# A twelve-sublayer decoder on one core: the normalised tile of every layer norm made by ScalarE from a scale and an offset instead of by VectorE

## What is computed

```python
def _layernorm(x, axis=-1, eps=1e-05):
    m = jnp.mean(x, axis=axis, keepdims=True)
    v = jnp.var(x, axis=axis, keepdims=True)
    return (x - m) / jnp.sqrt(v + eps)
...
x = x + _L0_attn_ref(_layernorm(x, axis=-1), L0_attn_w_qkv, L0_attn_w_out)
x = x + _L0_xattn_ref(ctx_1024, ctx_1024, _layernorm(x, axis=-1), L0_xattn_Wk, ...)
x = x + _L0_ffn_ref(_layernorm(x, axis=-1), ...)
... (L1, L2 and L3 in the same way)
```

## Time and profile before

| | |
|---|---|
| three timed runs | 4872.91, 4877.81, 4878.98 us (median 4877.81) |
| the profiled execution, and its span | 4866.22 us, span 4864.2 us |
| PE busy | 3539.3 us, 73% |
| DVE busy | 2997.2 us, 62% |
| ACT busy | 2028.7 us, 42% |
| POOL busy | 1241.7 us, 26% |
| mean granted TensorE clock | 0.833 |

### The profile page before, as it was taken

One profiled execution on the slowest core, in us unless ns is written; L12 is line 12 of the kernel. 1 busy time (PEld: TensorE's weight loads), 2 busy tenths in 40 slices (PEclk: granted clock), 3 DMA queues, 4 the chain that ended last, 5 costly groups with the idle time before them and its releaser, 6 DMA issues. The chain is left out here.

```text
span 4864.2 us, 69143 instructions
## 1 busy us (share of the span) xinstructions
PE 3539.3 (73%) x25546; PEld 2352.9 (48%) x25546; DVE 2997.2 (62%) x7047; ACT 2028.7 (42%) x3183; POOL 1241.7 (26%) x1568
## 2 busy tenths in 40 slices
PE   6768868566977787764886887866588788686655
PEld 4645545334665454432574554533366455453333
DVE  4535873885553785577555488377655558737834
ACT  2324445343343444444343354544433354453422
POOL 0001450550000333254000044145200014505500
PEclk7979989768988898877997998977799899887666
DMA  6020021313211012222212002122312100213121
GB/s 222 7 92 20 27 76 40 128 38 104 85 58 61 31 45 83 70 81 78 98 45 102 12 27 79 44 89 74 106 55 80 66 18 28 85 36 120 40 100 46
DMA packets 174903, 327.99 MB, mean 67 GB/s; under 512 B 13260, under 2 KB 114988, under 8 KB 173740
## 3 DMA queue, kind: packets, MB, share of 16 engines
q1 hardware_dynamic: 174572, 323.59, 19.5%
HBM read 231.87 MB, written 91.67 MB: 67 GB/s over the span
## 5 line engine op out<-in xcount | busy, mean ns | idle before, releaser
L1980 POOL TENSOR_TENSOR sb_big<-sb_big 128x512 f32<-128x512 f32 x384 | 497.7, 1310 | 275.7 <-DVE sb_big L2080 275.6
L1417 POOL TENSOR_TENSOR sb_rs<-sb_ve,sb_weights_const 128x4 f32<-128x4 f32 x112 | 113.7, 1015 | 1635.7 <-DVE sb_ve L1403 1635.7
L1864 PE MATMUL bank<-sb_big,sb_weights_const 128*128 128x512 f32 x512 | 373.4, 819 | 202.0 <-DVE sb_big L2102 201.4
L1941 ACT ACTIVATE bank<-sb_big,sb_Aneg 128x512 f32<-128x512 f32 x512 | 350.5, 687 | 391.9 <-DVE sb_big L2097 272.3
L2097 DVE TENSOR_TENSOR_SCAN sb_big<-bank,sb_big 128x512 f32<-128x512 f32 x384 | 465.2, 1212 | 4.7 <-POOL sb_big L1980 4.7
L1235 DVE TENSOR_REDUCE sb_small<-bank 128x4 f32<-128x308 f32 (+1 forms) x512 | 265.1, 524 | 318.0 <-PE bank L950 311.7
L971 PE MATMUL bank<-sb_big 128*77 128x128 bf16 (+1 forms) x2560 | 359.3, 232 | 124.7 <-issue 85.5
L971 PEld LDWEIGHTS bank<-sb_big 128*77 128x77 bf16 (+1 forms) x2560 | 272.7, 116 | 213.3 <-issue 148.3
L1120 ACT ACTIVATE sb_big<-bank 77x512 f32<-77x512 f32 (+1 forms) x352 | 208.3, 593 | 263.3 <-PE bank L992 173.8
L974 PE MATMUL bank<-sb_topT,sb_pick 128*77 128x128 bf16 (+1 forms) x2048 | 301.7, 228 | 0.0
L950 PE MATMUL bank<-sb_big 128*128 128x77 bf16 (+1 forms) x2048 | 186.3, 226 | 155.6 <-DMA sb_big<-query_parts 98.8
(11 more groups left out here) (339 smaller groups left out, 8174.2 us busy)
## 6 DMA issues: line engine op xcount, KB each, us to landing
sb_big<-query_parts SPq DMA_DIRECT2D x160, 512.0 KB, 6.6
sb_big<-state_rows SPq DMA_DIRECT2D x128, 512.0 KB, 3.8
query_parts<-sb_big SPq DMA_DIRECT2D x120, 384.0 KB, 3.3
sb_big<-key_parts SPq DMA_DIRECT2D x64, 512.0 KB, 9.0
sb_big<-context_key_parts SPq DMA_DIRECT2D x64, 308.0 KB, 3.8
key_parts<-sb_big SPq DMA_DIRECT2D x48, 384.0 KB, 4.4
context_key_parts<-sb_big SPq DMA_DIRECT2D x48, 231.0 KB, 4.1
sb_big<-masked_key_parts SPq DMA_DIRECT2D x32, 308.0 KB, 3.5
```

Source lines behind the costliest of these rows:

```text
L1864: pe.matmul(m.bank[s][2][:, :], m.const["ident"], M.h(s, 2 * (n % 2)), start=n == 0, stop=n == NS - 1)\
L1941: act.activation(M.dA(s, half), M.dl(s, half), ACT.Exp, scale=m.Aneg[:, NS * half + n:NS * half + n + 1])\
L1980: pool.tensor_tensor(M.h(s, 2 * (n % 2) + half), M.b_rows(s, n // 2)[:, n % 2, :], M.du(s, half), ALU.mult)\
```

## The change

DVE no longer makes the normalised tile and no longer waits for POOL. It stops after variance + eps. POOL gets two small products per norm: before the power it multiplies the mean by -1 (`m.minus`, a new constant tile), and after it, it multiplies that by the reciprocal deviation; this wants a wait of POOL on its own power. ACT makes the tile with four `Identity` activations, with the reciprocal deviation as scale and the product as bias, both pointers to a column. They stand in ACT's queue at the due time at which DVE had them (0.01, and 0.03 for the inner norms). The signals of the quantised network now go by the experts' names (`ff_`), which frees semaphores and moves nothing; POOL's set-up gets a memset and a wait.

```diff
-    yield 0.01 if made is None else 0.03
-    dve.wait_ge(*g.at("ln_rstd", key))
-    for b in range(NB):
-        last = dve.tensor_scalar(dst[s][:, b, :], src[s][:, b, :], m.mv[s][:, b, 0:1], m.rs[s][:, b:b + 1],
-                                 ALU.subtract, ALU.mult)
-    last.then_inc(*g.one("ln_xn", key))
 
 
 def norm_pool(pool, g, m, key):
     s = g.s
     yield 0.03 if key in (k + "i" for k in NESTED) else 0.01
+    pool.wait_ge(*g.at("ln_aggr", key))
+    pool.tensor_tensor(m.nm[s][:, :], m.mv[s][:, :, 0], m.minus[:, :], ALU.mult)
     pool.wait_ge(*g.at("ln_var", key))
     pool.tensor_tensor(m.rs[s][:, :], m.ve[s][:, :], m.const["neghalf"], ALU.pow)\
         .then_inc(*g.one("ln_rstd", key))
+    pool.wait_ge(*g.at("ln_rstd", key))
+    pool.tensor_tensor(m.nm[s][:, :], m.nm[s][:, :], m.rs[s][:, :], ALU.mult)\
+        .then_inc(*g.one("ln_off", key))
+
+
+def norm_act(act, g, m, key, src, dst, made=None):
+
+    s = g.s
+    yield 0.01 if made is None else 0.03
+    act.wait_ge(*g.at("ln_off", key))
+    for b in range(NB):
+        last = act.activation(dst[s][:, b, :], src[s][:, b, :], ACT.Identity, bias=m.nm[s][:, b:b + 1],
+                              scale=m.rs[s][:, b:b + 1])
+    last.then_inc(*g.one("ln_xn", key))
...
+                yield from norm_act(act, g, m, key, m.xin if key == "L0a" else m.x, m.xn)
                 if key in NESTED:
+                    yield from norm_act(act, g, m, key + "i", m.xn, inner, made=key)
...
+    pool.memset(m.minus[:, :], -1.0)
```

More of the change, by code:

```diff
@@ L204 @@
     x_upd="DVE has updated the residual", ln_stat="DVE: statistics", ln_aggr="DVE: mean and variance",
-    ln_var="DVE: variance + eps", ln_rstd="Pool: reciprocal deviation", ln_xn="DVE: normalised tile",
+    ln_var="DVE: variance + eps", ln_rstd="Pool: reciprocal deviation",
+    ln_off="Pool: minus the mean in deviations", ln_xn="ACT: normalised tile",
     ln_tr="PE: transposed normalised tile", ln_xT="ACT: it is in SBUF",
@@ L219 @@
     sc_in="Pool: a state's input", sc_y1="Pool: state added to the second half's y",
-    qf_pe="PE: quantised network", qf_a="ACT: quantised network", qf_d="DVE: quantised network",
-    qf_p="Pool: quantised network",
 )
@@ L266, in declare @@
     m.rs = [sb(f"rs{s}", [128, NB]) for s in range(STREAMS)]
+    m.nm = [sb(f"nm{s}", [128, NB]) for s in range(STREAMS)]
+    m.minus = sb("minus", [128, NB])
     m.small = [sb(f"small{s}", [128, 256]) for s in range(STREAMS)]
@@ L1425, in turn_pe @@
     if key == "L3f":
-        pe.wait_ge(*g.at("qf_d", "r3"))
+        pe.wait_ge(*g.at("ff_d", "r3"))
     else:
@@ L2222, in quantised_pe @@
         pe.matmul(m.bank[s][k][:, :], Q.w("w1", 128 * j, 128 * j + 128), m.xT[s][:, :], start=True, stop=True)\
-          .then_inc(*g.one("qf_pe", ("h", j)))
-        free[s, k] = ("qf_a", ("h", j))
+          .then_inc(*g.one("ff_pe", ("h", j)))
+        free[s, k] = ("ff_a", ("h", j))
     for b in range(NB + 1):
@@ L2234, in quantised_pe @@
                                     m.const["ident"])
-            last.then_inc(*g.one("qf_pe", ("tok", b)))
-            free[s, b % 2] = ("qf_d", ("q1", b))
+            last.then_inc(*g.one("ff_pe", ("tok", b)))
+            free[s, b % 2] = ("ff_d", ("q1", b))
         if b >= 1:
             yield Q.time(b - 1, 0.8)
-            pe.wait_ge(*g.at("qf_d", ("q3", b - 1)))
+            pe.wait_ge(*g.at("ff_d", ("q3", b - 1)))
             g.wait_free(pe, free, s, 2)
@@ L2243, in quantised_pe @@
                                     Q.qb(s, b - 1)[:, 128 * j:128 * j + 128], m.identb[:, :])
-            last.then_inc(*g.one("qf_pe", ("back", b - 1)))
-            free[s, 2] = ("qf_a", ("qT", b - 1))
+            last.then_inc(*g.one("ff_pe", ("back", b - 1)))
+            free[s, 2] = ("ff_a", ("qT", b - 1))
     yield 0.98
     g.wait_free(pe, free, s, 3)
-    pe.wait_ge(*g.at("qf_a", ("qT", NB - 1)))
+    pe.wait_ge(*g.at("ff_a", ("qT", NB - 1)))
     for b in range(NB):
@@ L2252, in quantised_pe @@
                              m.w2t[:, 128 * j:128 * j + 128], start=j == 0, stop=j == 3)
-    last.then_inc(*g.one("qf_pe", "out"))
+    last.then_inc(*g.one("ff_pe", "out"))
     free[s, 3] = ("x_upd", "L3f")
@@ L2260, in quantised_act @@
         yield 0.06 + 0.01 * j
-        act.wait_ge(*g.at("qf_pe", ("h", j)))
+        act.wait_ge(*g.at("ff_pe", ("h", j)))
         act.activation(Q.hp(s, j)[:, :, 1:T + 1], m.bank[s][j % 2][:, :].rearrange("p (b t) -> p b t", t=T),
-                       ACT.Copy).then_inc(*g.one("qf_a", ("h", j)))
+                       ACT.Copy).then_inc(*g.one("ff_a", ("h", j)))
     for j in range(4):
         yield 0.16 + 0.06 * j
-        act.wait_ge(*g.at("qf_d", ("conv", j, 2)))
+        act.wait_ge(*g.at("ff_d", ("conv", j, 2)))
         act.activation(Q.hs(s, j), Q.hs(s, j), ACT.Silu, bias=Q.w("convb", j, j + 1))\
-           .then_inc(*g.one("qf_a", ("hs", j)))
+           .then_inc(*g.one("ff_a", ("hs", j)))
     for b in range(NB):
         yield Q.time(b, 0.85)
-        act.wait_ge(*g.at("qf_pe", ("back", b)))
+        act.wait_ge(*g.at("ff_pe", ("back", b)))
         act.activation(Q.qT(s)[:, :, b * T:(b + 1) * T],
                        m.bank[s][2][:, :].bitcast(BF16)[:, 0:512].rearrange("p (j t) -> p j t", t=T),
-                       ACT.Copy).then_inc(*g.one("qf_a", ("qT", b)))
+                       ACT.Copy).then_inc(*g.one("ff_a", ("qT", b)))
 def quantised_pool(pool, g, m, Q):
@@ L2282, in quantised_pool @@
             last = pool.memset(Q.hp(s, j)[:, :, at:at + 1], 0.0)
-    last.then_inc(*g.one("qf_p", "pad"))
+    last.then_inc(*g.one("proj_p", "pad"))
 def quantise_tokens_dve(dve, g, m, Q):
@@ L2290, in step @@
     def step(name, last):
-        last.then_inc(*g.one("qf_d", name))
+        last.then_inc(*g.one("ff_d", name))
     def after(name):
-        dve.wait_ge(*g.at("qf_d", name))
+        dve.wait_ge(*g.at("ff_d", name))
     yield 0.02
@@ L2378, in quantised_dve @@
         if b >= 2:
-            dve.wait_ge(*g.at("qf_pe", ("back", b - 2)))
+            dve.wait_ge(*g.at("ff_pe", ("back", b - 2)))
         step("q3", dve.tensor_scalar(Q.qb(s, b), Q.qa(s, b), ROUND, None, ALU.subtract))
     yield 0.96
-    dve.reciprocal(Q.sm(s, 8), Q.sm(s, 7)).then_inc(*g.one("qf_d", "inv2"))
-    dve.wait_ge(*g.at("qf_d", "inv2"))
-    dve.tensor_scalar(Q.sm(s, 8), Q.sm(s, 8), m.wsc[:, 3:4], None, ALU.mult).then_inc(*g.one("qf_d", "f"))
+    dve.reciprocal(Q.sm(s, 8), Q.sm(s, 7)).then_inc(*g.one("ff_d", "inv2"))
+    dve.wait_ge(*g.at("ff_d", "inv2"))
+    dve.tensor_scalar(Q.sm(s, 8), Q.sm(s, 8), m.wsc[:, 3:4], None, ALU.mult).then_inc(*g.one("ff_d", "f"))
     yield 0.99
-    dve.wait_ge(*g.at("qf_d", "f"))
-    dve.wait_ge(*g.at("qf_pe", "out"))
+    dve.wait_ge(*g.at("ff_d", "f"))
+    dve.wait_ge(*g.at("ff_pe", "out"))
     for b in range(NB):
```

17 lines of the change are left out of this document (9 added, 8 removed).

## The result

The changed kernel takes 4931.6 us (4909.9 to 4945.9) where the kernel before takes 4875.4 us: a ratio of 1.0113, 95% interval 1.0070 to 1.0155, so 1.1% or some 55 us slower. Measured again beside the first experiments the ratio was 1.0115 (1.0098 to 1.0131). The forecast was 4965, the range 4900 to 5010: the sign is right, the time is in the range, the loss is 33 us smaller than forecast. The profiled execution took 4939.6 us (span 4937.7); against the one before (4864.2) the span grew by 73.5 us. A second profiled execution of the same kernel had a span of 4922.8. Two profiles of one program can lie 15 us apart: in the first of these PE was busy for 3546.3 us at a mean granted clock of 0.833, in the second for 3523.6 us at 0.839. Small sums over a trace are read with that in mind.

The account below looks back on a forecast made before the run. No engine is full; hand-overs between queues fixed at build time set the time. Five groups of places, 14 + 66 + 25 - 19 + 3 = 89 us, gave 4955 profiled, 4967 as median, taken as 4965; range 4900 to 5010.

Parts of the forecast that it names:

- 60 turns: Turns, of 96, at which PE was found to start within 0.2 us of the normalised tile's end.
- 17 places: Places with nothing of the other stream behind ACT's wait, each priced at the 0.83 us longer chain: 14 us.
- The price of the instructions: At each norm: second POOL product 0.31 us, four ACT activations 1.62 us, negation hidden where POOL is idle; chain 0.83 us longer.
- z: The end of POOL's power at a norm; tile forecast ready at z + 1.98, before at z + 1.15.
- Group 3: Six places where ACT's wait pushes back an activation needed by PE work ahead of the turn: 6 x 4.2 = 25 us.
- Group 4: 16 norms inside the scan, where the scan waits for DVE; relieving DVE gains 1.2 us each: -19 us.
- I keep half: At norms inside the scan, only 1.2 us of DVE's 2.5 us standstill was counted as gained.
- Groups 1, 2 and 5: Nothing of other stream behind, 14 us; table load or evacuation pushed back, 33 places, 66 us; other ten places, 3 us.
- only the chain grows: Rival: what ACT's wait pushes back has slack, only the longer chain costs; +44, 4922 us, chance 0.20.
- DVE was the hidden pace-maker: Rival: DVE's relief at norms lets the other stream's ready DVE work release PE; -46, 4832 us, chance 0.08.
- The delays breed: Rival: longer PE stops lower its clock and delays reach the other stream twice; 130 to 170, about 5025 us, chance 0.08.

Follow-up runs that it names:

- after_chain: Changed kernel with four more dependent POOL products before ACT's wait, so the tile comes 1.1 us later; ratio 1.0372 to the kernel before, +181 us.
- undo_two: Changed kernel, but DVE makes the tile as before at stream 1's L3a and stream 0's L1x; ratio 1.0047 to the kernel before, +23 us.
- scan_only: Kernel before, with ACT making the tile only at the four norms per pass inside the other stream's scan; 4826.4 us, ratio 0.9906, -46 us.
- rest_only: Changed kernel, but DVE makes the tile as before at the four scan norms and two costly norms per pass; ratio 1.0136 to the kernel before, +66 us.
- dve_hold: Kernel before, with DVE held 0.75 us after the tile by waiting for seven unused POOL products; ratio 1.0141, +69 us.
- block_only: Kernel before, with ACT held at the change's place by a wait and six small unused activations, old chain kept; ratio 1.0161, +79 us.
- act_late: Changed kernel with ACT's wait for most norms moved later in its queue (due 0.038); ratio 1.0064 to the kernel before, +31 us.
- scan_wait: Kernel with ACT's tile at the four scan norms only, but DVE's wait for the power kept there; ratio 0.9967 to the kernel before, -16 us.

## Why the prediction was right, and where its terms were off

*What bounds the kernel.* Right: hand-overs between fixed queues. It read too little into it, though. I followed the chain at 60 turns and called it pure at 17 places. The two kernels with a longer chain give 0.84 us a norm for 0.82 and 1.12 for 1.12, over all 112. A delay at a norm costs about its own length far beyond the places that I had called waiting. That isn't the chain by itself, though: DVE or ACT is held with it in these kernels, and in after_chain 26 to 49 of the 125 us are a slower TensorE.

*The price of the instructions.* Right: POOL's product 0.28 us with its hand-over (0.31 forecast), four activations 1.65 us (1.62), tile at z + 2.02 (z + 1.98), the negation hidden (the power starts 0.25 us after L1404, as it did after L1403).

*Group 3*, 25 us forecast. Mechanism and places right, undo_two makes it 33. The size was off at the place before L3a, read at 3.9 and found at some 6.4.

*Group 4*, -19 us forecast. This term was mis-sized: scan_only makes it -46, 2.9 us a norm in place of 1.2. The step that failed is "I keep half". The reason given for it (ACT's decay behind the norm) is real, 1.14 us in the row of scan_only, but POOL, the other half of the reason, did not hold the scan back: DVE waits for it, the norm's power aside, 12.9 us before and 13.6 in scan_only. In the traces PE stands idle 36 us less, 2.3 us a norm, so nearly the whole standstill of 2.5 us arrived. I have no row for the other 10 us; the executions of scan_only had a granted clock of 0.838 on average, the kernel before 0.833 on that chip.

*Groups 1, 2 and 5*, 14 + 66 + 3 = 83 us forecast. rest_only makes them 66. The order of things at the place of the earlier trace rows was as forecast, and the price of 2.0 us for a pushed-back evacuation can be right. The sum has no term for DVE's relief outside the scan. dve_hold shows that holding DVE 0.75 us longer costs 0.6 us a norm, nearly all of it away from the scans, so such a term can't be put at nothing without a reason; that the relief is what makes 66 of 83 is argued, not shown, and the interval of the 66 alone is 10 us either way. What is shown is that ACT's hold alone (block_only) costs as much away from the scans as the whole change. act_late says that ACT's later place doesn't help there: moved behind the other stream's work, these places lose as much.

*Sum.* By the runs -46 + 33 + 66 = 53 in place of 89. The 36 us are 27 from the scan and 17 from groups 1, 2 and 5, less 8 at group 3. Outside the scan the loss came to 99 us where 108 had been forecast; what moved the total was the gain in the scan, read at less than half. The range was wide enough to hold "only the chain grows" as well, so the total alone would not have told the two apart; undo_two and block_only do.

*The rivals.* "Only the chain grows" gave 4922, 10 us from the 4932 measured where the forecast was 33 off, but for the wrong reason: it prices the chain at 63 us and nothing for ACT's place, and undo_two and block_only show that the place costs. "DVE was the hidden pace-maker" was given 0.08 for the whole; as a mechanism it is shown at the four norms of the scan, where it wins; elsewhere only the reverse is shown, that holding DVE longer costs time. "The delays breed" (0.08) did not decide the change: PE's busy time there is 7 us above before in one trace and 16 below in the other. But a slower TensorE as part of a delay's price shows in after_chain and in scan_wait. The sign of the change depends on the place, and a cut of the sum by place would have shown that the part with a minus could be had alone.

*What would show it.* Four activations in 1.65 us: yes. They start 0.37 us after the power: yes. ACT up by 174 us and DVE down by 128: yes. ACT's wait for the product over 200 us: 252 + 23. PE waiting for L1133: 6.04 us at that place, twice the 3 forecast. The scan shorter: yes, PE's waits for it by 38 us. The prediction called itself wrong if DVE's relief showed as less idle time on PE outside the scan. It doesn't: away from the scans PE stands idle 690 us before and 774 with the change, and its waits for DVE other than for the tile fall only from 101 to 92 us.

## What to carry to other kernels

An engine that works in order pays for a wait twice: with its own time, and with what stands behind it in the queue. When a step moves from one engine to another, price the standstill at the wait as well as the instructions, on both engines; in the scan nearly the whole standstill of 2.5 us came back, not half. Then cut the sum by place: a change that loses 1.1% everywhere gained 0.9% where the engine it relieves sets the pace. And when two kernels differ by more than their waits do, compare the busy time of the same instructions: keeping DVE's wait cost 30 us, of which the traces show 7 as idle time and 18 as a slower TensorE.
